# First expert attention of a two-layer tower on one Trainium2 core: queries and keys as two products, another interleaving of two pairs of tiles

## What is computed

```python
h = h + ffn(_layernorm(h))               # x below is the normalised h
gate = softmax(relu(x @ Wg1 + bg1) @ Wg2 + bg2)
top_w, top_i = top_k(gate, 2); top_w = softmax(top_w)
q, k = split(x @ Wqk + bqk)              # three experts of 64 columns each
for e in range(3):
    v = x @ Wv[e] + bv[e]
    # expert 0: q goes through a 3-tap convolution along the tokens
    att = masked_softmax(q[e] @ k[e].T / 8)
    ys[e] = att @ v
out = concat(ys[e] * w[e]) @ Wp + bp     # w: top_w at its two experts, else 0
```

## Time and profile before

| | us |
|---|---|
| median of 3 runs | 2126.27 |
| lowest, highest | 2124.63, 2131.35 |
| profiled execution, its time | 2131.68 |
| profiled execution, its span | 2130.0 |
| busy in the span: PE, DVE, ACT, POOL | 1599.1, 1313.0, 977.8, 400.1 |

### The profile page before, as it was taken

The page is one execution under the profiler, slowest core; times in us unless marked ns, Lnnn a source line. Parts: engine busy times, 40 slices in busy tenths (PEclk is TensorE's granted clock), DMA queues, the critical chain, the costliest instruction groups (busy, mean ns, idle before and its releaser), DMA issues.

```text
span 2130.0 us, 35436 instructions
## 1 busy us (share of the span) xinstructions
PE 1599.1 (75%) x12060; PEld 1166.6 (55%) x12060; DVE 1313.0 (62%) x4361; ACT 977.8 (46%) x2773; POOL 400.1 (19%) x494
## 2 busy tenths in 40 slices
PE   0166765966777568888888768888888859999996
PEld 0032224855555445555555546666666637777775
DVE  7898885877777777778878735555555531221221
ACT  1367998833333445554554423333333314434342
POOL 7302331000000100000000001222122223333332
PEclk9985555578777679999999968777777769999998
DMA  3000001089900000000000000000000027777775
GB/s 71 14 1 1 1 1 20 3 162 191 178 5 0 1 1 1 0 0 0 0 0 0 1 25 12 24 23 19 15 22 22 23 82 185 173 178 184 175 177 133
DMA packets 136262, 112.99 MB, mean 53 GB/s; under 512 B 29417, under 2 KB 128457, under 8 KB 136137
## 3 DMA queue, kind: packets, MB, share of 16 engines
q1 hardware_dynamic: 119320, 91.70, 18.4%
q0 software_dynamic: 16864, 20.33, 5.0%
HBM read 69.19 MB, written 45.94 MB: 54 GB/s over the span
## 4 chain that ended last, share of the span: by engine, by line
PE 54%; DVE 26%; ACT 13%; issue 4%; POOL 1%; DVEq 0%; DMA 0%; another core or an unknown queue 0%; ACTq 0%; POOLq 0%; SPq 0%
ACT bank L716 8%; PE bank L2323 8%; PE bank L1007 7%; PE bank L2308 5%; PE bank L2312 4%; PE bank L1988 3%; PE bank L966 3%; PE bank L1219 2%; PE bank L1000 2%; PE bank L1666 2%; PE bank L2001 2%; DVE WK L1840 1%; DVE WK L1582 1%; DVE R L1582 1%; DVE R L1840 1%
## 5 line engine op out<-in xcount | busy, mean ns | idle before, releaser
L1047 POOL TENSOR_TENSOR WK<-WK,mhalf 128x2 f32<-128x2 f32 (+1 forms) x96 | 77.9, 812 | 906.0 <-DVE WK L1506 326.9
L2360 ACT ACTIVATE R<-bank,R 128x256 f32<-128x256 f32 x234 | 98.3, 471 | 217.0 <-PE bank L2312 217.0
L2212 DVE SCALAR_TENSOR_TENSOR WK<-bank,R,WK 128x192 f32<-128x192 f32 x78 | 28.9, 413 | 264.1 <-PE bank L2323 264.1
L1007 PE MATMUL bank<-WK,R 96*128 96x256 f32 x576 | 177.5, 465 | 15.9 <-ACT WK L973 11.0
L716 ACT ACTIVATE bank<-bank,nbias,sc 128x128 f32<-128x128 f32 x384 | 168.9, 954 | 20.5 <-POOL nbias L528 20.5
L2241 POOL DMA_INDIRECT moe_sum<-WK x78 | 121.5, 1558 | 257.6 <-DVE WK L2212 190.5
L2323 PE MATMUL bank<-R 128*128 128x192 f32 x936 | 169.1, 331 | 0.0
L716 ACT ACTIVATION_READ_ACCUMULATOR bank<-bank,nbias,sc 128x1 f32 x384 | 162.5, 729 | 0.0
L2323 PEld LDWEIGHTS bank<-R 128*128 128x128 f32 x936 | 150.1, 190 | 13.3 <-issue 13.3
L1007 PEld LDWEIGHTS bank<-WK,R 96*128 96x128 f32 x576 | 130.9, 237 | 43.5 <-ACT WK L973 15.6
L966 PE MATMUL bank<-ident,WK 128*96 128x128 f32 x320 | 67.2, 348 | 85.3 <-DVE WK L1030 68.7
(11 more groups left out here) (493 smaller groups left out, 3936.3 us busy)
## 6 DMA issues: line engine op xcount, KB each, us to landing
moe_rows_in<-zeros SPq DMA_DIRECT2D x1, 25026.0 KB, 139.4
R<-in_L_ffn_w SPq DMA_DIRECT2D x39, 576.0 KB
R<-in_L_ffn_w SPq DMA_DIRECT2D x39, 384.0 KB
R<-moe_rows_in SPq DMA_DIRECT2D x39, 194.0 KB, 4.5
R<-in_L_ffn_w SPq DMA_DIRECT2D x78, 96.0 KB
R<-in_L_ffn_b SPq DMA_DIRECT2D x39, 96.0 KB
moe_sum<-resid POOLq DMA_DIRECT2D x16, 192.0 KB
moe_sum<-WK POOLq DMA_INDIRECT x78, 5.8
```

What stands on the lines that cost most here:

```text
L1007: mm = nc.tensor.matmul(out, w[0:C, c, m], a.xT[0:C, c, :], start=(c == 0), stop=(c == 1))
L1047: nc.gpsimd.tensor_tensor(a.rs[:, 0:n], a.ve[:, 0:n], mhalf[:, 0:n], ALU.pow).then_inc(f.root, 1)
L2360: ins = nc.scalar.activation(x_hid[q], bank[(0, 2, 0)[p] + n][:, 0:NR], ACT.Gelu, bias=xb_1[h][:, q:q + 1])
```

## The change

It has three parts. On PE, queries and keys of experts 0 and 1 become two products with a signal each: the queries right behind the transposes, into bank 3, the keys behind expert 2's product, into bank 0. The older pair's steps stand between the newer pair's products: tile 0's attention is transposed between the value product of tile 0 and that of tile 1, and tile 1's transposes, the product with the values and the whole projection now stand ahead of expert 2's product, with the projection waiting for each tile's copy apart. On ACT, queries are copied by an instruction of their own and keys last; the gate's first exponential stands ahead of the copies of expert 2 and keys, the second one ahead of all six score exponentials. On DVE, the gate's softmax and its two best (nine short instructions) stand ahead of the norm, where tile 0's scores stood, and both tiles' scores stand behind it. No arithmetic is added or removed.

```diff
@@ -1131,7 +1131,7 @@
             normalised(v, a, f, tiles_of(g, a), a.x, per(g, 1, 1)).then_inc(f.x, 1)
             yield
 
-            v.wait_ge(f.qk, per(g, 2, 1))
+            v.wait_ge(f.qk, per(g, 3, 1))
             q0 = a.qkT[0:HE, 0, :].rearrange("p (t n) -> p t n", t=M)
             qc = a.qc[0:HE, :].rearrange("p (t n) -> p t n", t=M)
             ch.step(nc.vector.tensor_scalar(qc, q0, f_conv[0:HE, 1:2], f_convb[0:HE, 0:1], ALU.mult, ALU.add))
@@ -1155,17 +1155,6 @@
 
         def vector_f_2(v, ch, g, a, f):
 
-            for i in range(M):
-                v.wait_ge(f.scores, per(g, M, i + 1))
-                for b, at in (((0, slice(0, 3, 2)), (1, slice(1, 2))), ((2, slice(0, 1)), (3, slice(1, 3))))[i]:
-                    n = 2 if at in (slice(0, 3, 2), slice(1, 3)) else 1
-                    ins = nc.vector.scalar_tensor_tensor(
-                        out=a.s[:, i, at, :], in0=a.bank[b][:, 0:n * P].rearrange("p (e n) -> p e n", e=n),
-                        scalar=HE ** -0.5, in1=f_mask.unsqueeze(1).to_broadcast([P, n, P]), op0=ALU.mult, op1=ALU.add)
-                ch.step(ins)
-                nc.vector.tensor_reduce(a.nm[:, i, :], a.s[:, i], X, ALU.max, negate=True).then_inc(f.rowmax, 1)
-                if i == 0:
-                    yield
             v.wait_ge(f.gate_exp, per(g, 2, 1))
             ch.step(nc.vector.tensor_reduce(a.m4, a.ge, X, ALU.add))
             ch.step(nc.vector.reciprocal(a.m4, a.m4))
@@ -1179,6 +1168,17 @@
             nc.vector.tensor_tensor(a.we[:, :, 1], a.cmp[:, 0, :], a.cmp[:, 2, :], ALU.max)
             ch.step(nc.vector.tensor_scalar(a.m4, a.cmp[:, 2, :], -1.0, 1.0, ALU.mult, ALU.add))
             ch.step(nc.vector.tensor_tensor(a.we[:, :, 2], a.cmp[:, 1, :], a.m4, ALU.max))
+            yield
+
+            for i in range(M):
+                v.wait_ge(f.scores, per(g, M, i + 1))
+                for b, at in (((0, slice(0, 3, 2)), (1, slice(1, 2))), ((2, slice(0, 1)), (3, slice(1, 3))))[i]:
+                    n = 2 if at in (slice(0, 3, 2), slice(1, 3)) else 1
+                    ins = nc.vector.scalar_tensor_tensor(
+                        out=a.s[:, i, at, :], in0=a.bank[b][:, 0:n * P].rearrange("p (e n) -> p e n", e=n),
+                        scalar=HE ** -0.5, in1=f_mask.unsqueeze(1).to_broadcast([P, n, P]), op0=ALU.mult, op1=ALU.add)
+                ch.step(ins)
+                nc.vector.tensor_reduce(a.nm[:, i, :], a.s[:, i], X, ALU.max, negate=True).then_inc(f.rowmax, 1)
             v.wait_ge(f.gate_exp, per(g, 2, 2))
             ch.step(nc.vector.tensor_tensor(a.we, a.we, a.ge, ALU.mult))
             ch.step(nc.vector.tensor_reduce(a.m4, a.we, X, ALU.add))
@@ -1211,13 +1211,13 @@
             pe.wait_ge(f.x, per(g, 1, 1))
             turn(a, a.x, 0, f.xTp)
             pe.wait_ge(f.xT, per(g, 1, 1))
-            for o, b in enumerate((0, D)):
-                mm = product(a, fw_qk, slice(b, b + P), a.bank[3][:, o * NM:(o + 1) * NM])
-            mm.then_inc(f.qk_p, 1)
+            product(a, fw_qk, slice(0, P), a.bank[3][:, 0:NM]).then_inc(f.qk_p, 1)
             for i in range(M):
                 for c in range(2):
                     mm = nc.tensor.matmul(a.bank[2][:, i * VG:(i + 1) * VG], a.xT[0:C, c, i * P:(i + 1) * P],
                                           fw_vg[0:C, c, :], start=(c == 0), stop=(c == 1))
+                if i == 0:
+                    yield
             mm.then_inc(f.v_p, 1)
             yield
             for o, b in enumerate((P, D + P)):
@@ -1226,9 +1226,9 @@
                         mm = nc.tensor.matmul(a.bank[1][HE * i:HE * (i + 1), o * P:(o + 1) * P], fw_qk[0:C, c, b:b + HE],
                                               a.xT[0:C, c, i * P:(i + 1) * P], start=(c == 0), stop=(c == 1))
             mm.then_inc(f.qk_p, 1)
-            yield
-
-            pe.wait_ge(f.qk, per(g, 2, 2))
+            product(a, fw_qk, slice(D, D + P), a.bank[0][:, 0:NM]).then_inc(f.qk_p, 1)
+
+            pe.wait_ge(f.qk, per(g, 3, 3))
             pe.wait_ge(f.conv, per(g, 1, 1))
             pe.wait_ge(f.v, per(g, 1, 1))
             lo, hi = slice(0, HE), slice(HE, P)
@@ -1256,43 +1258,40 @@
                                      stop=True)
                 nc.tensor.matmul(b[HE * i:HE * (i + 1), P:2 * P], a.vv[:, i, 2 * HE:D], a.pt[:, i, 2, :], start=True,
                                  stop=True).then_inc(f.y_p, 1)
-            yield
-            pe.wait_ge(f.y, per(g, M, M))
-            for i in range(M):
+            for i in range(M):
+                half = slice(HE * i, HE * (i + 1))
+                pe.wait_ge(f.y, per(g, M, i + 1))
                 nc.tensor.matmul(a.bank[2 * i][:, 0:D], a.y[:, i, :], fw_p[:, 0, :], start=True, stop=False)
-            for i in range(M):
-                half = slice(HE * i, HE * (i + 1))
                 nc.tensor.matmul(a.bank[2 * i][:, 0:D], a.y[half, 2, :], fw_p[half, 1, :], start=False,
                                  stop=True).then_inc(f.proj_p, 1)
+            yield
 
         def scalar_f_1(act, g, a, f):
             act.wait_ge(f.xTp, per(g, 1, 1))
             take_turned(a, 0, a.xT, f.xT)
             yield
-            act.wait_ge(f.qk_p, per(g, 2, 1))
-            for o in range(2):
-                ins = nc.scalar.activation(a.qkT[:, o, :], a.bank[3][:, o * NM:(o + 1) * NM], ACT.Identity,
-                                           bias=fb_qk[:, o:o + 1])
-            ins.then_inc(f.qk, 1)
-            yield
-            act.wait_ge(f.qk_p, per(g, 2, 2))
+            act.wait_ge(f.qk_p, per(g, 3, 1))
+            nc.scalar.activation(a.qkT[:, 0, :], a.bank[3][:, 0:NM], ACT.Identity, bias=fb_qk[:, 0:1]).then_inc(f.qk, 1)
+            yield
+            act.wait_ge(f.gate_in, per(g, 2, 1))
+            nc.scalar.activation(a.ge, a.gt, ACT.Exp).then_inc(f.gate_exp, 1)
+            act.wait_ge(f.qk_p, per(g, 3, 2))
             for o in range(2):
                 ins = nc.scalar.activation(a.qkT[:, 2 + o, 0:P], a.bank[1][:, o * P:(o + 1) * P], ACT.Identity,
                                            bias=fb_qk[:, 2 + o:3 + o])
             ins.then_inc(f.qk, 1)
-            act.wait_ge(f.gate_in, per(g, 2, 1))
+            act.wait_ge(f.qk_p, per(g, 3, 3))
+            nc.scalar.activation(a.qkT[:, 1, :], a.bank[0][:, 0:NM], ACT.Identity, bias=fb_qk[:, 1:2]).then_inc(f.qk, 1)
+
+        def scalar_f_2(act, g, a, f):
+            act.wait_ge(f.gate_in, per(g, 2, 2))
             nc.scalar.activation(a.ge, a.gt, ACT.Exp).then_inc(f.gate_exp, 1)
-
-        def scalar_f_2(act, g, a, f):
             for i in range(M):
                 act.wait_ge(f.rowmax, per(g, M, i + 1))
                 for e in range(TE):
                     s = a.s[:, i, e, :]
                     ins = nc.scalar.activation(s, s, ACT.Exp, bias=a.nm[:, i, e:e + 1], accum_out=a.rsum[:, i, e:e + 1])
                 ins.then_inc(f.exp, 1)
-                if i == 0:
-                    act.wait_ge(f.gate_in, per(g, 2, 2))
-                    nc.scalar.activation(a.ge, a.gt, ACT.Exp).then_inc(f.gate_exp, 1)
             yield
             for i in range(M):
                 act.wait_ge(f.turned_p, per(g, M, i + 1))
```

More of the change, by code:

```diff
@@ L1258, in tensor_f_2 @@
                                  stop=True).then_inc(f.y_p, 1)
-            yield
-            pe.wait_ge(f.y, per(g, M, M))
-            for i in range(M):
-                nc.tensor.matmul(a.bank[2 * i][:, 0:D], a.y[:, i, :], fw_p[:, 0, :], start=True, stop=False)
             for i in range(M):
                 half = slice(HE * i, HE * (i + 1))
+                pe.wait_ge(f.y, per(g, M, i + 1))
+                nc.tensor.matmul(a.bank[2 * i][:, 0:D], a.y[:, i, :], fw_p[:, 0, :], start=True, stop=False)
                 nc.tensor.matmul(a.bank[2 * i][:, 0:D], a.y[half, 2, :], fw_p[half, 1, :], start=False,
                                  stop=True).then_inc(f.proj_p, 1)
+            yield
         def scalar_f_1(act, g, a, f):
```

## The result

| | before | changed |
|---|---|---|
| median, us (4 runs each) | 2128.81 | 2103.84 |
| lowest, highest | 2124.63, 2132.18 | 2099.46, 2107.98 |
| profiled execution, its span | 2130.0 | 2106.3 |
| stage of the first expert attention in it | 285.6 | 259.2 |
| mean of 14 combined steps | 17.04 | 15.41 |

The ratio is 0.9885, with an interval of 0.9868 to 0.9903: about 25 us faster. The time lies inside the predicted range, but above the 2088 to 2100 that the forecast itself was given, and the gain is 25 where the forecast had 34. The stage's length is taken from its first layer-norm statistics (L1019) to its last reset on DVE (L1068), a step from one pair's statistics to the next pair's. The stage became 26.5 us shorter; 1.3 us ahead of it and 1.4 us behind it differ the other way, in code that is the same in both.

What follows compares the result with a forecast made beforehand. A chain going round between PE and DVE bounds the 17.04 us step; floor 14.3 plus 0.4 (values) and 0.2 (exponentials) gives 14.9, over 15 steps 32.1, plus 1.8 for the first step: 2092 us, range 2080 to 2112, forecast's own 2088 to 2100.

Steps and rivals of the forecast that it cites:

- rival C: PE's products, now cut by waits, raise the clock later; slow 17.1 us steps alternate with 14.9: 2108.9 us, chance 0.15.
- DVE's floor of 14.3 us: Combined step on DVE: its length if DVE never waits, since the change takes nothing off DVE, 14.3 us.
- The values' wait: DVE behind the convolution: waits for tile 1's value product at the slow clock, 0 to 0.7 us, mean 0.4 a step.
- The first single step: Stage's first step: with the keys behind, values come 1.8 us sooner, and the next step starts that much sooner.
- the projection: PE to DVE's residual add: tile 0's ready 1.75 us behind the last transpose, at 12.6 to 14.75; DVE arrives at 14.1.
- the slow time line: PE up to the projection at 1.2 GHz, counted from the residual add's start: tile 1's transposes end at 13.0 us.
- The exponentials: ACT's score exponentials for DVE's weights and scaling: a DVE wait of 0 to 0.35 us, priced at 0.2 a step.
- Rival B: PE's shorter pause keeps the clock at 2.4 GHz, DVE never waits, 14.3 us a step: 2083.4 us, chance 0.17.
- the idle stretch ahead of the turning: PE ahead of transposing the normed rows (L966): idle time falls from 4.1 us to 2 to 3.3 us a step.
- D: PE stays at 1.2 GHz through every step and becomes the bound, 17.6 to 17.7 us a step: 2133.7 us, chance 0.06.
- The wait ahead of L1199: Sign on DVE: its idle time until the projection is done falls from 1.83 us to below 0.5 a step.
- ACT waits ahead of expert 2's copy: Sign on ACT: it waits for DVE's gate input, at 14.1 us, before copying expert 2, at no cost to DVE.

Runs made afterwards that it cites:

- e9: Changed kernel plus three matmuls with unused results ahead of PE's wait for the norm: ratio 0.9766 to before, mean step 14.25 us.
- e5: The changed kernel itself, run again on a second chip: ratio 0.9883 to before, mean step 15.36 us.
- e1: Changed kernel plus two matmuls with unused results ahead of PE's wait for the norm: ratio 0.9812 to before, mean step 14.34 us.
- e2: Kernel before plus eight matmuls with unused results ahead of PE's wait for the norm: ratio 0.9830 to before, mean step 15.00 us.
- e4: Changed kernel with the projection in its old order, both tiles' first halves, then both second halves: ratio 0.9914 to before, mean step 15.82 us.
- e6: Changed kernel with the keys' product back behind the queries' and both copied there: ratio 0.9957 to before, mean step 16.84 us.
- e3: Changed kernel with the gate's part undone on DVE and ACT, PE's order still changed: ratio 0.9948 to before, mean step 16.47 us.
- e7: Kernel before with only the gate's part of the change added: ratio 0.9987 to before, mean step 17.13 us.
- e10: Changed kernel with the projection in its old order and four extra matmuls: ratio 0.9817 to before, mean step 15.04 us.

## Why the prediction was right, and where it was off

**Right in sign and mechanism.** The chain between the projection and the norm was cut, the transposes and the projection moved ahead, and the time came in inside the range. But that range was wide enough for rival C. The measured 2103.84 us misses the forecast's own 2088 to 2100, and it is nearer to C's 2108.9 than to 2092. DVE's floor of 14.3 us is near what e9 measured (14.25, of which 0.15 is waiting). The values' wait was given as 0.4 us in the mean and up to 0.7; it is 5.8/14 = 0.41, up to 0.8. The first single step was to bring 1.8 us; it went from 13.82 to 11.95, 1.87; that this fits so well is partly luck, since e5's first step of 12.50 makes it 1.3.

**The term that was mis-sized is the projection.** I had it 1.75 us behind tile 1's last transpose and so ready about when DVE arrives, with no term in the sum. In the slow step shown above the transposes end at 579.44, which is 13.3 us behind the residual add's start and near the 13.0 of the slow time line; DVE's next add starts at 581.97, 2.5 us later. Tile 0's copy behind the product with the values (L1303) does not only stand in ACT's queue, as I had it; it waits for that product (L1259), whose first matmuls ran at the lower clock. On ScalarE in the changed kernel:

```profile
580.34 0.28 ACT L1303 ACTIVATE R<-bank 128x128 f32<-128x128 f32 x1 [0.37 <-PE bank L1259]
```

and behind it the projection has 1.04 us for a tile (L1264 at 580.82, two matmuls 0.52 apart), not the 0.7 that I took as half of four matmuls in the old order, where the two second halves overlap. DVE's wait for the projection is thus 9.0/14 = 0.64 us a step. The exponentials, which I gave 0.2, cost 0.2/14, nothing. The sum corrected is 14.3 + 0.41 + 0.64 = 15.35, and 15.41 was measured. (With e9's floor, 14.25 - 0.15 = 14.10, it is 15.15, and 0.26 us stay without a term; 0.20 of them is DVE's busy time, 177.18 us against 174.33 in e9.) Over 15 steps the 0.5 us make up the 7.4 us by which the stage's gain of 26.5 falls short of 33.9; the remaining 1.5 us of the missing gain lie outside the stage.

**Rival B was the more valuable one.** I gave the held clock 0.17 and 2083 us. It did not happen by itself: the idle stretch ahead of the turning shrank to 1.4 us a step (I had said 2 to 3.3), and the clock fell all the same. The pause of 0.7 us for ACT's copy lies close behind it, and the two may act together, but no run takes that pause away, so this is not shown. Made to happen, it gives what B said, in stage and step (e1, e9). The Trainium skill, "TensorE: Matmul & The Clock Gate", section "Why this matters for your kernels", asks for short pauses between bursts of matmuls. In kind e1, e2 and e9 agree: with the pause filled the mean granted clock went from 0.83 to 0.96 and 0.98, and from 0.79 to 0.95. But a shorter pause alone was not enough here: the changed kernel's longest wait ahead of the turning is 1.9 us, against 4.4 before, and its clock fell in every step.

**C and D.** The clock was not down for longer than before: in the step of the earlier trace rows from about 584.1 to 590.8, in the step shown here from about 573.2 to 579.9, in the next for half of that. So the interleaving with waits did not keep it down, against C's reason. C's picture of slow steps alternating with fast ones did come, with 16.37 us instead of 17.1 for the slow and 14.35 instead of 14.9 for the fast. PE's list became no bound, against D. But e4, e6 and e3 are steps of C's size, 15.8 to 16.8 us: a little more delay at one place is enough to get there.

**What I said would show it.** The wait ahead of L1199 fell to 0.64, not below 0.5; the steps are 14.35 and 16.37 instead of 14.3 to 15.2; ACT waits ahead of expert 2's copy, but for PE's product (31.4 us), not for DVE's gate input; PE waits for the keys' copy as forecast (0.56 us in the step shown); DVE does not wait for scores, though behind a fast step they end only 0.9 us before it wants them (score products from 569.75 for 0.9 us, DVE's first at 571.64), where I had given them over 1.7.

## What to carry to other kernels

Where a chain goes round between two engines, first ask what clock the products on it run at: here the cheapest edit, a few matmuls without use in a 4 us pause, was worth 30 us of stage in the old order, more than the reordering, and the two together 43. Moving work behind a consumer (keys late) needs the consumer moved too (scores behind the norm): the gate's part alone brought nothing (e7), and without it 7 of the 26 us of stage were left (e3). And fill a pause only where it is one: four extra matmuls at the lower clock in front of work that was ready held it up by 3 us (e10).

The fastest kernel that computes everything is e9, which beats both: 0.9766 of before against the changed kernel's 0.9885; 17.1 us of that against the changed kernel are in the stage. e1, with two matmuls, has the same stage within 0.6 us, and the two ratios are not told apart clearly.

## What was not expected of the hardware

- The clock and the step seem to hold each other. Before, a slow and a fast step took 34.1 us together, with the gate part alone 34.14 (17.25 and 16.89), though PE waited 0.84 us longer a step; the changed kernel took 30.72, and with 0.59 us less work on DVE 30.73. Less work on one engine came out as longer waits, until the clock was held.
- Less work on PE made the step longer (e4, 15.82 against 15.41 us) beside a lower granted clock. The mechanism is not settled.
- The part of the program behind the stage, the same in all kernels, varied by 12 us on one chip (1364.4 us in e2, 1376.9 in e4). What it depends on is open; executions of one and the same kernel on one chip differ as much (e9's four take 2054.3 to 2066.0 us). A gain of a few us in this stage can be hidden or doubled by it.
